# ScalarE's order in the attention stage: the tanh of the shared expert's gate ahead of the softmax's exponential

## What is computed

```
h  = layernorm(x)
q, k, v = h Wq + bq, ctx Wk + bk, ctx Wv + bv            # 16 heads of 16
x  = x + softmax(mask(q k^T / 4)) v Wo + bo
z  = layernorm(x)
scores = sigmoid(z gate_weight^T)                        # 32 experts, 8 groups of 4
chosen = top 6 of the best 4 groups by scores + bias;  weights = 2.5 * chosen scores / their sum
routed = sum over the 6 of weight * (silu(z gate_e) * (z up_e)) down_e
shared = (silu(z Wsg) * (z Wsu)) Wsd                     # 256 hidden features
out = x + routed + shared
```

## Time and profile before

| what | value |
|---|---|
| three runs, median (lowest to highest) | 807.11 us (792.71 to 819.54) |
| profiled execution | 796.54 us |
| its span | 794.7 us |
| TensorE's mean granted clock | 0.974 |
| busy share of the span, TensorE matmuls | 92% |
| VectorE, ScalarE, GpSimd | 66%, 49%, 67% |
| first stage | to about 398 us |

### The profile page before, as it was taken

The page is one execution under the profiler, slowest core; times in us unless marked ns, Lnnn a source line. Parts: engine busy times, 40 slices in busy tenths (PEclk is TensorE's granted clock), DMA queues, the critical chain, the costliest instruction groups (busy, mean ns, idle before and its releaser), DMA issues.

```text
span 794.7 us, 18389 instructions
## 1 busy us (share of the span) xinstructions
PE 728.0 (92%) x5864; PEld 655.6 (82%) x5864; DVE 526.8 (66%) x1628; ACT 389.1 (49%) x836; POOL 534.6 (67%) x778
## 2 busy tenths in 40 slices
PE   6899999999999999996879999999899999999970
PEld 3788888888888888885669999899798899889960
DVE  5988767777777776776734227667576576657663
ACT  2454444544444455420046666656465565656640
POOL 0127767787878887878600028788877888898875
PEclk9999999999999999999999999999999999999995
DMA  9323334434332233334565558789788788877853
GB/s 267 102 61 114 126 120 127 127 103 133 132 128 79 81 107 122 132 127 139 168 199 186 174 184 247 244 259 273 237 250 248 236 259 256 255 253 243 255 184 111
DMA packets 97294, 140.13 MB, mean 176 GB/s; under 512 B 14943, under 2 KB 69731, under 8 KB 97200
## 3 DMA queue, kind: packets, MB, share of 16 engines
q1 hardware_dynamic: 77112, 87.50, 34.4%
q0 software_dynamic: 18432, 50.36, 20.6%
q10 hardware_dynamic: 1656, 1.10, 0.5%
HBM read 75.98 MB, written 62.94 MB: 175 GB/s over the span
## 4 chain that ended last, share of the span: by engine, by line
PE 55%; issue 16%; DVE 11%; POOL 6%; ACT 4%; DMA 3%; another core or an unknown queue 2%; SPq 1%; DVEq 0%; ACTq 0%; POOLq 0%
PE sc_ps L992 15%; PE bank L1004 8%; PE bank L805 5%; PE sc_ps L865 4%; PE sc_ps L976 4%; PE bank L793 3%; POOL rows L513 3%; PE sc_ps L771 3%; PE bank L751 2%; PE bank L826 2%; PE sc_ps L767 2%; DVE work L1481 2%; DVE work L1462 2%; POOL work L503 2%
## 5 line engine op out<-in xcount | busy, mean ns | idle before, releaser
L992 PE MATMUL sc_ps<-work 128*128 128x128 f32 x1792 | 220.3, 276 | 3.0 <-DVE work L1481 1.0
L992 PEld LDWEIGHTS sc_ps<-work 128*128 128x128 f32 x1792 | 209.9, 192 | 5.0 <-ACT work L655 2.7
L550 POOL DMA_INDIRECT work<-yrows,dest x192 | 189.2, 985 | 36.1 <-POOL work L503 17.7
L513 POOL DMA_INDIRECT rows<-work,dest x192 | 188.0, 979 | 36.2 <-issue 29.6
L503 POOL MEMSET work<- 128x304 f32 (+1 forms) x350 | 133.4, 381 | 94.9 <-DMA yrows<-work 83.1
L1004 PE MATMUL bank<-wdn,work 128*128 x448 | 117.8, 386 | 17.0 <-DVE work L1436 15.4
L1436 DVE TENSOR_TENSOR work<-work,sc_ps 128x256 f32<-128x256 f32 x112 | 46.9, 419 | 124.9 <-ACT work L660 57.2
L1004 PEld LDWEIGHTS bank<-wdn,work 128*128 128x128 f32 x448 | 76.6, 191 | 26.1 <-issue 20.1
L681 ACT ACTIVATE work<-bank 128x512 f32<-128x512 f32 x112 | 66.9, 597 | 51.7 <-PE bank L1004 30.4
L655 ACT ACTIVATE work<-sc_ps 128x512 f32<-128x512 f32 x112 | 66.6, 595 | 42.0 <-PE sc_ps L976 36.2
L1462 DVE SCALAR_TENSOR_TENSOR work<-work 128x256 f32<-128x256 f32 x160 | 76.8, 480 | 15.0 <-DMA work<-yrows,dest 8.2
(11 more groups left out here) (168 smaller groups left out, 1097.5 us busy)
## 6 DMA issues: line engine op xcount, KB each, us to landing
work<-rows SPq DMA_DIRECT2D x224, 128.0 KB
yrows<-work SPq DMA_DIRECT2D x112, 256.0 KB
wgu<-in_egu SPq DMA_DIRECT2D x16, 512.0 KB
store<-in_x SPq DMA_DIRECT2D x8, 512.0 KB, 12.1
wdn<-in_edn SPq DMA_DIRECT2D x8, 512.0 KB
rows<-padrow SPq DMA_DIRECT2D x8, 512.0 KB
out<-work SPq DMA_DIRECT2D x32, 128.0 KB
rows<-work,dest POOLq DMA_INDIRECT x192
```

Of the source, the lines that this page charges most:

```text
L513: pool.indirect_dma_start(rows[:, :], bass.IndirectOffsetOnAxis(ap=dest[:, t, k:k + 1], axis=0), rowb[:, m, :], None).then_inc(scat[m], 16)
L550: pool.indirect_dma_start(yg[:, g % RG, :], None, yrows[0:2 * n * P, :], bass.IndirectOffsetOnAxis(ap=dest[:, t, k:k + 1], axis=0)).then_i ...
L992: last = mm(ps8[2 + m % 2][:, (2 * w + g) * P:(2 * w + g + 1) * P], wst[w][m % 2][:, k * 2 * I + g * I:k * 2 * I + (g + 1) * I], xeT[:, m ...
```

## The change

In ScalarE's list the call of `half_tanh` moves up by three places, from behind `ev_x2T` to ahead of `exps`. Nothing else is edited: the same instructions with the same operands run on every engine, and only ScalarE's order differs, in each step that has both.

```diff
             def step(tile):
                 at_tile(tile, 2, ev_pT(1))
+                at_tile(tile, 5, half_tanh)
                 at_tile(tile, 1, exps)
                 at_tile(tile, 0, ev_q)
                 at_tile(tile, 4, ev_x2T)
-                at_tile(tile, 5, half_tanh)
                 at_tile(tile, -1, norm1)
```

## The result

The changed kernel takes 836.64 us in the median of four runs (830.09 to 839.3), the kernel before 803.64 us beside it (four runs, 792.71 to 819.54): 33.0 us more. The ratio is 1.045, with a 95% interval of 1.040 to 1.050: slower, as forecast. That is more than the 19 us of the likeliest case and above that case's own 818 to 833 us, but inside the whole range of 799 to 842. The profiled execution of the changed kernel has a span of 837.5 us.

A forecast was written before the change was run, and what follows sets the result against it. The first stage was taken as bound by a chain of projection's signal, tanh, two products, scores and TensorE's order. Steps of 11.28 against 10.51 us, 0.77 x 25 = 19.3 us, gave 807.1 + 19 = 826 us; range 799 to 842.

The forecast's parts named there:

- likeliest case: First stage: signal at T + 8.45, step 11.28 us against 10.51, 19 us more in all; chance 0.42.
- a: Time of the shared projection's signal, which the tanh waits for; taken as 0.02 us ahead of a tanh that waited.
- T': Start of the next tile's score matmuls; forecast a + 2.83 with the change, against a + 1.46 before.
- T: Start of a tile's score matmuls (L767) in the first stage, from which times in a step are counted.
- the price's chain: Signal, tanh, exponential to row copy's end, L842, next scores: a + 2.83, 1.37 us more behind the same signal.
- (b): Rival: the signal takes the first release, T + 7.7; step 10.53 us, no change, 807 us; chance 0.25.
- two release points in the scatters' cycle: TensorE's signals go out at 0.7 or, by guess, 1.45 us into the scatters' cycle of 1.49 us.
- (a): Rival: the signal stays as late relative to T; about 1.2 us a step, 30 us, 837 us; chance 0.20.
- (c): Rival: TensorE's new pause frees the signal, T + 7.15; step 9.98 us, 13 us saved, 794 us; chance 0.08.
- (d): Rival: nothing visible changes because the exponential isn't on the chain; 807 us; chance 0.05.

The follow-up runs named there:

- e5: The changed kernel itself, unedited, run again on another chip beside the kernel before: 767.34 us against 763.45, ratio 1.005.
- e10: The kernel before, with the projection's signal given late, by a later matmul of TensorE: 839.26 us, ratio 1.048 to the kernel before.
- e9: The changed kernel, with the projection's signal given late, by a later matmul of TensorE: 891.95 us, ratio 1.113 to the kernel before.
- e3: The changed kernel with 14 small filler matmuls a step on TensorE: 784.18 us, ratio 1.031 to the kernel before.
- e2: The changed kernel with the row copy moved ahead of the tanh on ScalarE: 770.68 us, ratio 1.013 to the kernel before.
- e4: The changed kernel with the shared expert's projections ahead of the output projection on TensorE: 764.33 us, ratio 1.001 to the kernel before.
- e7: The changed kernel without GpSimd's scatters, SyncE writing the same bytes to fixed rows: 758.55 us, ratio 0.993 to the kernel before.
- e8: The kernel before without GpSimd's scatters, SyncE writing the same bytes to fixed rows: 751.65 us, ratio 0.985 to the unedited kernel before.

## Why the prediction was right, and where it was off

**The direction and the mechanism.** That the tanh can't start before its signal, that the exponential then waits behind it, and that VectorE's wait for the tanh is no prize, all hold: 25 of 25 tanh wait, the exponential starts 0.30 us behind a, and T' - a is 2.92 us where 2.83 was worked out. A step at full clock takes 11.36 us in the mean of twelve, forecast 11.28.

**The placing of a was right by luck.** In eleven of the twelve steps at full clock a lies between T + 8.38 and T + 8.53, forecast 8.45, but by two errors that cancel. I had the sixth scatter start at T + 7.02 and the signal go out 1.45 us later. It starts at T + 7.79 (209.68 in the step shown), and the signal goes out 0.70 us behind it. The round of six was to start on VectorE's variance; it starts on L1262, made from the ranks, in all 25 steps (in 12 before), and the ranks wait for q, the link that is missing from the price's chain too. The twelfth step, 10.75 us long, took the release of rival (b), with a at T + 7.76. The reading of two release points in the scatters' cycle fared better: thirteen of the 25 signals come 0.62 to 0.72 us behind a scatter's start and seven 1.40 to 1.45; the other five, in steps with a lower clock, are 0.02 us behind their modelled end, 0.9 to 2.5 us after the sixth scatter's start.

**The term that was mis-sized.** The step "11.28 against 10.51: 0.77 x 25 = 19.3 us" sets a step at full clock against a mean that holds slower ones. Before, 22 steps at full clock took 10.36 us in the mean and three with a lower clock 11.58; after, 12 take 11.36 (136.4 us in all) and 13 take 12.28 (159.7 us), with a clock between 0.75 and 0.93. So 25 x (11.36 - 10.36) = 25 us are the later chain, and 13 x 0.92 - 3 x 1.22 = 8 us are TensorE's clock, which I had left out: a mean of 0.91 over 296 us is 2 x 0.09 x 296 = 53 us at half clock, against 2 x 0.02 x 263 = 11 before.

**What the lower clock goes with.** TensorE now pauses at L852 in 19 of the 25 steps, eleven times for 0.5 to 0.8 us and eight times for 1.4 to 1.5, 18.4 us in all, and its clock falls 11 times; seven of the eight long pauses have a fall during them or up to 2.3 us behind them. Before, it paused nine times for 0.4 to 0.8 us, 4.7 us in all, and the clock fell three times. In e5 there is no pause over 0.25 us and no fall; in e10, 19 pauses, 20.5 us in all, and 9 falls; in e9, 25 pauses of 1.5 us and 24 falls. On chip 12 the mean clock of whole executions is 0.96 to 0.97 in the kernel before, 0.93 to 0.95 in e10 and 0.91 in e9. So the clock goes with the pauses, in either order of ScalarE's list, and lateness put in by hand lowers it. The experiment meant to fill the pauses, e3, doesn't show it, so that filling them would give the clock back is not shown.

**The price's chain was named wrongly.** I took L842's wait for the row copy as the link that closes the chain. e2 shows it isn't: the rank matmul's wait for q closes it, 1.49 us at L852. The two sums agree by accident, 0.28 + 2.02 + 0.15 + 0.36 there and 0.28 + 1.74 + 0.14 + 0.74 here, both behind the 0.02 of the tanh's start.

**The rivals.** (a), a as late as before, had the nearest time (837 us), but not the mechanism: in the steps at full clock a moved, from T + 9.0 in the mean of those that waited to T + 8.4. It is the steps with a lower clock, a at T + 9.2 in the mean, that bring the sum near to (a)'s. (b) and (c) give the first release and no delay; the latter is what chips 6 and 11 show, at a = T + 7.03. There the change costs 4 us and does not gain the 13 us of (c), because without late signals the kernel before has no mean step of 10.51 us to improve on but TensorE's own 9.96 (248.90/25). (c) let the delay go in the changed kernel alone, and that mistake could have been seen. (d) is out. How much of the forecast fits is up to the chip: on one like chip 11 its 19 us would have been wrong.

**What stays open.** Why TensorE's signals come late on some chips. Before the first scatter they were prompt in the first measurement too (tile 0's tanh starts 0.04 us behind the modelled end there in the changed kernel), and each late one falls at one of two places in the scatters' cycle, so the scatters seem to take part there; but on the other two chips the same scatters delay nothing, so they are not enough. The run without scatters was not made on a chip with late signals. Each chip was used at one time only, so the chip and its state at that time are not told apart. Nor were fillers in the right place tried there, nor e4's order, which might be faster than both kernels on such a chip; on the others no kernel with all of its work beat the one before.

## What to carry to other kernels

An instruction that waits for a signal must stand on its in-order engine behind everything that is ready earlier and wanted by others: compare the arrival of its own signal with the start of what it would overtake, not how long its consumer waits for it. Read the arrival from the start of an instruction that was idle for it; the modelled end of a matmul was up to 2.3 us too early here (the kernel before, first measurement). And lay the waits of the whole queue behind the moved instruction down to guards of shared PSUM banks, since a guard far from the change closed the chain.

## What was not expected of the hardware

The kernel before took 764.10 and 763.45 us in the median on two chips (761 to 773 on the two) and 802.59 on a third, where the first measurement had 803.64. In the first stage the cause shows in the trace: on the fast chips the tanh of the changed kernel, waiting for the projection in all 25 steps, starts 0.04 us after the modelled end of its matmuls in the step shown of e5, and TensorE's clock is 1.00 between tile 6's and tile 31's scores; in the first measurement it starts 1.49 us after it in the step shown above, and the clock is 0.91 (in the kernel before, 1.00 on chip 11 and 0.98 in the first measurement). The second stage, whose work and order all edits but e7's and e8's leave alone, takes 376 to 380 us from its first transposes to the end in the profiles of the fast chips, and 392 to 405 in the others. So one and the same reordering cost 0.5% on one chip and 4.5% on another.
